# A causal attention and mixture-of-experts block: softmax sums of four key tiles added on GpSimd, weights' high parts rounded on ScalarE, and all eight PSUM banks handed out by one planner

## What is computed

```python
def attention(x):                                  # x: 2 x 1024 x 128
    q = (x @ wq).reshape(B, T, 2, 4, 128)
    k_lat = (x @ wk_down).reshape(B, T, 2, 32); v_lat = (x @ wv_down).reshape(B, T, 2, 32)
    k = einsum('bkhl,ld->bkhd', k_lat, wk_up);     v = einsum('bkhl,ld->bkhd', v_lat, wv_up)
    scores = einsum('bqhrd,bkhd->bhrqk', q, k) * 128 ** -0.5
    probs = softmax(where(causal, scores, finfo.min), axis=-1)
    return einsum('bhrqk,bkhd->bqhrd', probs, v).reshape(B, T, 1024) @ wo

def ffn(x):                                        # 32 experts of 64, 16 anchors of 32, one shared of 64
    weights = top6_of_two_of_four_groups(sigmoid(x @ gate.T) + bias)
    routed = sum over experts of weight * (silu(x @ w_gate) * (x @ w_up)) @ w_down
    return routed + shared(x) + 0.1 * anchor_of_first_choice(x)

x = x + layernorm(attention(layernorm(x)))
x = x + layernorm(ffn(layernorm(x)))
```

## Time and profile before

| what | us |
|---|---|
| median of 3 runs | 415.49 |
| the three runs | 418.74, 415.49, 414.37 |
| the profiled execution's own time | 416.28 |
| its span, first to last instruction | 414.2 |
| PE busy (share of the span) | 393.9 (95%) |
| DVE busy | 281.5 (68%) |
| POOL busy | 275.7 (67%) |
| ACT busy | 231.4 (56%) |
| PE's share of the chain that ended last | 77% |

### The profile page before, as it was taken

One profiled execution on the slowest core, in us unless ns is written; L12 is line 12 of the kernel. 1 busy time (PEld: TensorE's weight loads), 2 busy tenths in 40 slices (PEclk: granted clock), 3 DMA queues, 4 the chain that ended last, 5 costly groups with the idle time before them and its releaser, 6 DMA issues.

```text
span 414.2 us, 7003 instructions
## 1 busy us (share of the span) xinstructions
PE 393.9 (95%) x2168; PEld 260.5 (63%) x2168; DVE 281.5 (68%) x711; ACT 231.4 (56%) x450; POOL 275.7 (67%) x338
## 2 busy tenths in 40 slices
PE   8998999998999999999998999999999999999993
PEld 8664555553454644444556778767887788778871
DVE  5985897882857885526347776678765686557665
ACT  4555355564545466664675455865556655665643
POOL 6124867975976498473667886498963988477651
PEclk9989999998999999999999999999999999999997
DMA  7347090083230050500000000001000000000000
GB/s 215 52 108 169 16 220 13 0 196 52 40 38 3 2 77 3 71 9 2 3 0 2 1 1 2 0 0 28 1 1 2 25 2 0 1 2 25 0 2 25
DMA packets 9906, 14.56 MB, mean 35 GB/s; under 512 B 1232, under 2 KB 5520, under 8 KB 9488
## 3 DMA queue, kind: packets, MB, share of 16 engines
q1 hardware_dynamic: 9584, 13.49, 15.7%
q10 hardware_dynamic: 288, 0.64, 0.5%
HBM read 6.26 MB, written 1.05 MB: 18 GB/s over the span
## 4 chain that ended last, share of the span: by engine, by line
PE 77%; POOL 7%; DVE 6%; ACT 4%; issue 3%; DMA 2%; SPq 1%; POOLq 0%; DVEq 0%; ACTq 0%
PE ps L1240 9%; PE ps L1242 9%; PE ps L1241 9%; PE ps L1354 9%; PE ps L1333 9%; PE acc L1368 8%; PE total L1378 5%; PE acc L1439 4%; PE acc L1441 4%; PE acc L1440 4%; POOL silu L839 3%; DMA qst<-q_lo 2%; PE ps L1336 2%; PE ps L1356 1%; PE ps L1388 1%
## 5 line engine op out<-in xcount | busy, mean ns | idle before, releaser
L839 POOL TENSOR_TENSOR silu<-silu,cwb 128x512 f32<-128x512 f32 x80 | 102.5, 1292 | 40.3 <-ACT silu L971 35.8
L1095 DVE TENSOR_REDUCE nmax_h<-ps 128x1 f32<-128x512 f32 (+3 forms) x152 | 92.3, 655 | 47.8 <-PE ps L1336 24.3
L940 ACT ACTIVATE probs<-ps 128x512 f32<-128x512 f32 (+1 forms) x152 | 80.0, 579 | 70.2 <-PE ps L1354 43.7
L759 POOL TENSOR_TENSOR probs<-probs 128x768 f32<-128x768 f32 (+2 forms) x48 | 78.0, 1644 | 34.0 <-ACT probs L940 21.2
L1172 DVE TENSOR_TENSOR h_lo<-ps,h_hi 128x512 fp32r<-128x512 f32 (+1 forms) x84 | 57.0, 686 | 23.8 <-ACT h_hi L981 23.2
L1167 DVE TENSOR_TENSOR ps<-silu,ps 128x512 f32<-128x512 f32 (+1 forms) x84 | 57.9, 693 | 22.3 <-POOL silu L839 17.5
L971 ACT ACTIVATE silu<-ps 128x512 f32<-128x512 f32 x80 | 47.5, 597 | 45.5 <-PE ps L1242 39.7
L1333 PE MATMUL ps<-kst,qst 96*128 96x512 f32 (+3 forms) x192 | 63.8, 386 | 4.0 <-ACT probs L940 1.9
L1240 PE MATMUL ps<-xT_hi,w_hi 128*128 128x512 f32 x164 | 65.4, 399 | 1.3 <-ACT silu L971 1.3
L1242 PE MATMUL ps<-xT_hi,w_lo 128*128 128x512 f32 x164 | 64.4, 393 | 0.0
L1241 PE MATMUL ps<-xT_lo,w_hi 128*128 128x512 f32 x164 | 64.4, 393 | 0.0
(11 more groups left out here) (191 smaller groups left out, 518.7 us busy)
## 6 DMA issues: line engine op xcount, KB each, us to landing
qst<-q_hi SPq DMA_DIRECT2D x14, 256.0 KB, 5.6
qst<-q_lo SPq DMA_DIRECT2D x7, 256.0 KB, 6.1
x_sb<-in_attn_x SPq DMA_DIRECT2D x4, 256.0 KB, 6.5
raw<-in_ffn_w_gate SPq DMA_DIRECT2D x1, 1024.0 KB, 4.9
raw<-in_ffn_w_up SPq DMA_DIRECT2D x1, 1024.0 KB, 6.4
raw<-in_ffn_w_down SPq DMA_DIRECT2D x1, 1024.0 KB, 5.0
kst<-k_hi SPq DMA_DIRECT2D x6, 128.0 KB, 3.7
result<-x_sb SPq DMA_DIRECT2D x3, 256.0 KB, 2.3
```

The source lines that it names most:

```text
L759: nc.gpsimd.tensor_tensor(into, into, probs[:, k % KTBUF, js, cols], ALU.add).then_inc(added, 1)
L839: nc.gpsimd.tensor_tensor(silu[:, k % HRING, :], silu[:, k % HRING, :], cwb[:, m % 2, t // ET, :], ALU.mult).then_inc(scaled_ready, 1)
L940: nc.scalar.activation(probs[:, k % KTBUF, j:j + w, at:at + cols], bank(full)[:, 0:w * cols].rearrange("p (w c) -> p w c", w=w), ACT.Exp). ...
L1095: nc.vector.tensor_reduce(nmax_h[:, n % 2, i, j:j + w, h], bank(full)[:, 0:w * keys].rearrange("p (w k) -> p w k", w=w), AX.X, ALU.max, ne ...
```

## The change

Six edits go together.

1. POOL adds in sums of four tiles: tiles 1, 2 and 3 of each run of four are added one after the other onto tile 0 (`SUM_FROM`, `first_of`, `last_of`), still in two halves of two heads (`PARTS`). There are 72 add instructions instead of 48, and 12 groups of ones products instead of 24.
2. The buffer of a sum's first tile is held until its ones products are done; the other three rotate (`buffers()`, `BUF`, `WAS`, `LEFT`).
3. The high parts of the weights are rounded by ACT (`whi`), and POOL only subtracts. The split of the down weights runs through the tiles backwards, and only its last three steps (`t < OVER_K`) wait for the keys.
4. `acc` and `total` are gone: all eight banks are common, and the sums of `pv`, `ones` and `down` get theirs from the planner like every other step.
5. silu, `hi` and `lo` of the first three units wait for the buffer under them alone, and `g` 0 no longer waits for the last exponential.
6. In the planner one rank of the routing of chunk 0 is 4.5 instead of 5.5, and POOL's costs are set anew, so the order changes nearly everywhere.

```diff
-BANKS = 6
+BANKS = 8
+SUM_FROM = {TPC: (0,), 2 * TPC: (0, TPC)}
+PARTS = ((0, 2), (2, REP))
-WSPLITS = range(0, MT, 3)
+WSPLITS = [list(range(0, MT, 3)), list(range(0, MT, 3)), list(range(0, MT, 3))[::-1]]
+OVER_K = 2 * CH // P
+def first_of(n, kt):
+    return max(f for f in SUM_FROM[kts(n)] if f <= kt)
+def buffers():
+    held, at, was = [None] * KTBUF, {}, {}
+    turn = list(range(KTBUF))
+    for n in range(NB):
+        for kt in range(kts(n)):
+            own = turn.pop(0)
+            if kt == first_of(n, kt):
+                first = own
+            else:
+                turn.append(own)
+            at[n, kt], was[n, kt], held[own] = own, held[own], (n, kt)
+            if kt == last_of(n, first_of(n, kt)):
+                turn.append(first)
...
-ROUTE_RANK = (5.5, 100, 121, 142)
+ROUTE_RANK = (4.5, 100, 121, 142)
...
-                    into = probs[:, (k - 1) % KTBUF, js, cols]
-                    pool.wait_ge(pv_done, PV["pv", n, kt - 1])
+                    into = probs[:, BUF[n, f], j:end, cols]
+                    pool.wait_ge(pv_done, PV["pv", n, f])
...
+                    if kt > f + 1:
+                        pool.wait_ge(added, ADD["add", n, kt - 1, part])
...
-                        link(nc.gpsimd.tensor_copy(w_hi[:, a, ts, :], w_raw[:, ts, :]))
-                        nc.gpsimd.tensor_tensor(w_lo[:, a, ts, :], w_raw[:, ts, :], w_hi[:, a, ts, :].bitcast(F32), ALU.subtract).then_inc(split_done, 1)
...
+                    pool.wait_ge(w_hi_ready, W_HI["whi", a, t])
...
+                elif kind == "whi":
+                    _, a, t = ev
+                    if a < 2:
+                        act.wait_ge(gu_w_in, 16 * (4, 6)[a])
+                    else:
+                        act.wait_ge(down_w_in, 16 * 3)
+                    if a == 2 and t < OVER_K:
+                        act.wait_ge(k_in[NCH - 1], 16 * 3)
+                    for rows, ts in weight_tiles(a, t):
+                        hi = w_hi[:, a] if a < 2 else wd_hi
+                        last = nc.scalar.activation(hi[0:rows, ts, :], w_raw[0:rows, ts, :], ACT.Copy)
+                    last.then_inc(w_hi_ready, 1)
...
-                    if k == 0:
-                        act.wait_ge(pv_done, len(PV))
-                        act.wait_ge(ones_done, len(ONES))
                     if k >= HRING:
                         act.wait_ge(h_ready, H["h", k - HRING])
+                    else:
+                        rows_left(act, k)
```

More of the change, by code:

```diff
@@ L109, in p2_steps, with parts_of, last_of @@
     return out
-def halves_of(ev):
-    return {j // 2 for j in range(ev[3], ev[3] + ev[4])}
+def parts_of(ev):
+    return {part for part, (j, end) in enumerate(PARTS) if ev[3] < end and j < ev[3] + ev[4]}
+def first_of(n, kt):
+    return max(f for f in SUM_FROM[kts(n)] if f <= kt)
+def last_of(n, f):
+    return max(kt for kt in range(kts(n)) if first_of(n, kt) == f)
+def buffers():
[11 more added lines that the diff above has]
+                turn.append(first)
+    name = {own: k for k, own in enumerate(turn)}
+    return {x: name[own] for x, own in at.items()}, was, [held[own] for own in turn]
 WARM = 14
@@ L208, in chunk_of, with leaves @@
         return CPB * b + c
+    def leaves(user):
+        if user is None:
+            return []
+        n, kt = user
+        return [("ones", n, kt)] if kt == first_of(n, kt) else [("pv", n, kt), *(("add", n, kt, part) for part in range(len(PARTS)))]
     step("SP", ("x_load",), 320, 0)
@@ L300, in plan @@
             step("PE", ev, max(19, own * w * 23 // CH) + 25 * masked, rank, ("s_dma", n), b and ("unit_rows",), bank=1, until=("exp", *ev[1:]))
[L301 to L306 removed]
+            step("ACT", ("exp", *ev[1:]), 22 + w * own * 80 // 1000, rank, ev, *leaves(WAS[n, kt]))
@@ L317, in plan @@
-        step("DVE", ("recip", n), 170, n + 2, ("ones", n, kts(n) - 2))
+                step("PE", ("pv", n, kt), 10 + cols * 17 // 100, rank - 0.2, *exps, *vs, kt and ("pv", n, kt - 1),
+                     bank=0 if kt else 1, until=("yl", n))
+                f = first_of(n, kt)
+                for part, (j, end) in enumerate(PARTS):
+                    if kt > f:
+                        step("POOL", ("add", n, kt, part), 18 + (end - j) * cols * 215 // 1000, rank - 0.1, ("pv", n, f),
+                             *[e for e in exps if part in parts_of(e)], kt > f + 1 and ("add", n, kt - 1, part))
@@ L318, in plan @@
+                if kt == last_of(n, f):
+                    step("PE", ("ones", n, f), 10 + (CH - first_col(n, f)) * 17 // 100, rank - 0.15, *(("add", n, kt, part) for part in range(len(PARTS))),
+                         f and ("ones", n, first_of(n, f - 1)), bank=0 if f else 1, until=("recip", n))
+        step("DVE", ("recip", n), 170, n + 2, ("ones", n, first_of(n, kts(n) - 1)))
         step("DVE", ("yl", n), 70, n + 2, ("recip", n), ("pv", n, kts(n) - 1), n >= GROUPS and ("post_out", n // GROUPS - 1))
@@ L390, in plan @@
     return o, o.settle()
-KT_AT = [(n, kt) for n in range(NB) for kt in range(kts(n))]
-KT = {at: k for k, at in enumerate(KT_AT)}
+BUF, WAS, LEFT = buffers()
 PLACED, PLAN = plan()
@@ L424 @@
 MUL = count("POOL", "mul")
[L425 removed]
+W_HI = count("ACT", "whi")
 LN = {ev: k for k, ev in enumerate(MOM)}
@@ L541, in tiles, with sums, rows_left, weight_tiles @@
             return ap.rearrange("p (t d) -> p t d", d=D)
+        def sums(m):
+            return bank(("down", MT * m))
+        def rows_left(engine, row):
+            n, kt = LEFT[row // REP]
+            engine.wait_ge(pv_done, PV["pv", n, kt])
+            if kt == first_of(n, kt):
+                engine.wait_ge(ones_done, ONES["ones", n, kt])
+            else:
+                engine.wait_ge(added, max(ADD["add", n, kt, part] for part in range(len(PARTS))))
+        def weight_tiles(a, t):
+            if a == 0:
+                return [(P, slice(t, min(MT, t + 3)))]
+            return [(P, slice(t, min(SHARED, t + 3)))] + ([(SI, slice(SHARED, MT))] if a == 2 and t + 3 >= MT else [])
         def tail_tiles(half):
-            return tiles((total if half else bank(("tail_T", 0)))[:, 0:CH // 2])
+            return tiles(bank(("tail_T", half))[:, 0:CH // 2])
         def normed_of(ev):
```

157 lines of the change are left out of this document (69 added, 88 removed).

## The result

The change made the kernel slower: 425.25 us median (422.56 to 428.07, four runs) against 414.93 us of the kernel before beside it. The two medians have the quotient 1.025; the ratio on record is 1.0206, with a 95% interval of 1.0143 to 1.0268, so the kernel is slower by more than 1%, and whether by more than 2% stays open. Some executions of one kernel lie over 1.5% above its fastest, at a lower granted clock; a ratio compares without them, a median has them in, so the two can differ. The forecast was 409.9 us, the range ended at 418.5. The profiled execution took 422.56 us, its span is 420.3 us.

The account below looks back on a forecast made before the run. PE was taken to bound the kernel, as long as nothing makes it wait. From the profiled 416.28 us, -8.6 + 5.4 - 1.0 - 1.4 - 0.8 = -6.4 us gave 409.9 us; range 404 to 418.5 us.

Parts of the forecast that it names:

- Adds: POOL's extra adds of probabilities: 39.7 us more work over the kernel, 29.4 us of it in blocks 2 to 5.
- The balance in blocks 2 to 5: POOL's 106.7 us of work plus 8.4 us of waits against PE's 109.7 us: PE loses 5.4 us.
- The third rival: Slower: a sum's fourth-tile exponential waits for the previous sum's last add and ones group; 428.4 us, chance 0.12.
- Ones groups: PE's ones products: twelve of 24 groups go, 8.56 us less, 6.3 us of it in blocks 2 to 5.
- Casts: Weight rounding: POOL loses 3.7 us in blocks 2 to 5; ACT gets 10.3 us, covered by its idle time.
- Block 4's queries and the half clock: PE's 1.66 us wait before block 4's scores plus 1.5 us of slow clock: 1.0 us won taken.
- The fourth rival: ACT's wait for the last keys costs the full 6.9 us instead of winning 1.0: 417.8 us, chance 0.04.
- Start of the experts: First silu of the experts waits for tile 1's buffer only: 1.4 us less, bounds 0 and 3.0.
- Eight banks: Common banks among the experts give g and u more room ahead: 0.8 us less, bounds 0 and 3.2.

Follow-up runs that it names:

- e1: Changed kernel in the same order, with nm's low part made by a reduction over one tile instead of a two-tile VectorE subtraction: 413.12 us, ratio 0.990.
- e2: e1 with the routing comparisons above and ties moved from VectorE to GpSimd, in a new planner order: 405.58 us, ratio 0.971.
- e6: e2 with the planner's landing times for queries and keys raised, which makes a new order: 401.70 us, ratio 0.959.
- e14: e6 with sums of two tiles instead of four: 406.29 us, ratio 0.975.
- e15: e6 run once more, unchanged, on another chip: 404.71 us, ratio 0.972.
- e7: e2 with sums of two tiles instead of four: 411.34 us, ratio 0.983.
- e4: Changed kernel with sums of two key tiles as before the change, its other parts kept: 408.28 us, ratio 0.977.
- e11: e4 with rounding of the weights' high parts back on GpSimd: 406.09 us, ratio 0.974.
- e5: e2 with three down-weight roundings over the keys' buffer put behind block 3's fifth exponential: 408.75 us, ratio 0.975.
- e10: Changed kernel with the rank of chunk 0's routing steps back at 5.5 instead of 4.5: 430.60 us, ratio 1.031.
- e13: e11 with the experts' first silu behind the last pv and ones group again, as before the change: 407.30 us, ratio 0.975.
- e16: Kernel before the change with e6's landing times in its planner, nothing else: 410.75 us, ratio 0.988.

## Why the prediction was wrong

**The step that failed is "Adds".** It priced an add as time on GpSimd only, and "The balance in blocks 2 to 5" let GpSimd reach PE by its pace only. The price per instruction was right (1.276 us measured for 512 elements, 1.292 taken; 24, 16, 16 and 16 adds), and GpSimd's busy time in the stretch was 105.73 us where 106.7 was worked out. What was missing is what a busy GpSimd does to another engine: VectorE's instructions with two inputs in SBUF stand while GpSimd's run. In the trace before, `nm` and `above` took 0.47 us at most in the attention, where they met pauses or short steps of GpSimd; with the pauses filled, four of them took 1.7 to 6.3 us in blocks 2 to 5. The stretch took 127.8 us against the 120 named as the mark of failure; VectorE's waits and the half clock behind them are worth 3.1% (e1) and up to another 1.9% (e2, where the order changes too). The Trainium skill, SBUF — State Buffer (section "Who interferes with whom"), states it: a VectorE instruction with two SBUF inputs contends with a GpSimd instruction that reads SBUF, the first holds an exclusive lock and the other fully blocks, while `tensor_reduce` never contends. By that rule, e1 agrees on who blocks (0.19 us for the reduction). On how long, the page has the whole instruction of the holder; here that fits the shorter waits (1.68 us at 36.23), while the costly ones went through up to seven instructions in a row (6.63 us), and the measurement decides.

**The third rival** had the right side (slower) and the wrong mechanism, and that its 428.4 us lie near the 425.25 measured is luck. Its loop of buffers is there unchanged in e1 and e2, which are 3 and 5% faster than the changed kernel; the 0.4 us that PE waits for GpSimd's sums says the same. The chance of 0.12 for slower was too low, and the mechanism that came had no chance at all.

**Ones groups**: right, 96 records, all of 512 queries, and 13.7 us busy instead of 22.0, so 8.3 us less where 8.6 were taken. **The balance**: right in kind once VectorE no longer meets the adds. GpSimd needs 106.7 us in e6, as worked out, and PE could do it in 108.1 - 6.3 = 101.8 us, not 109.7. So by this estimate 6.9 us are given back where 5.4 were taken, a net of -8.6 + 6.9 = -1.7 us against -3.2 in the sum. e14 and e15 show 1.6 us and e7 and e2 5 us, so the size is known to a few microseconds only, and that the first agrees so well is luck. **Casts**: right in size, ScalarE's roundings cost nothing that e4 and e11 can tell.

**Block 4's queries and the half clock**: the sign was wrong, and the cause too. 1.0 us of gain was taken; the stall grew from 1.66 to 2.9 us, with a half clock behind it as before. The prediction held the queries' last part for what came late. The trace before says that it was the keys:

```profile
89.74 0.76 SPq L658 DMA_DIRECT2D kst<-k_lo  x1
...
kst<-k_lo SPq DMA_DIRECT2D x1, 128.0 KB, 7.9
```

They landed at 89.74 + 7.9 = 97.6, and PE went on at 97.89; the queries' last part took 8.4 us from 87.76 and was there 1.5 us earlier. In the changed kernel the keys were issued at 88.42 and took 7.5 us, and PE went on at 96.09. So the load of the down weights, out of the way as forecast, was of little account (0.4 us), and PE came to the wait 3.0 us earlier (93.2 instead of 96.2).

**The fourth rival**: ScalarE's wait for the keys was there (4.0 us) and held nobody in the changed kernel's order, by e5; in e10's order it cost PE a stall of 3.8 us. **Start of the experts**: 1.4 us taken. PE's waits for silu 0 are gone from the trace after, but undoing the edit cost nothing that the runs can tell (e11 to e13). **Eight banks**: mis-sized, 0.8 us taken. With the order that came along e13 shows 2.5%, some 10 us; another order alone was worth 5 us to the kernel before (e16).

## What to carry to other kernels

An engine's idle time is not free if another engine needs it to be idle: before GpSimd is filled, list VectorE's instructions that read two SBUF tiles, however small, and see who waits behind them. A 16-column subtraction there stood for up to 6.6 us and stopped PE with it, and written as a reduction over one tile it took 0.19 us. And a planner that takes 2.2 and 3.3 us for landings that take 4.9 to 7.5 does not see a stall of 3 us that four numbers remove; whether the time falls with it has to be measured.
